# Second attention: DVE instead of ACT copies each pair's output out of PSUM, first in every odd slot

## The reference, cut to what matters

```
scores = jnp.einsum('bhqd,bhkd->bhqk', q, k_h) / math.sqrt(HEAD_DIM)
scores = jnp.where(causal[None, None], jnp.finfo(scores.dtype).min, scores)
attn = jax.nn.softmax(scores, axis=-1)
ctx = jnp.einsum('bhqk,bhkd->bhqd', attn, v_h)
ctx = ctx.transpose(0, 2, 1, 3).reshape(b, t, D_OUT)
```

## Time and profile before

| | us |
|---|---|
| median of three runs | 1215.43 |
| the profiled execution | 1214.89 |
| its span in the trace | 1213.3 |
| PE busy in the span | 1180.8 (97%) |
| PEld busy | 1023.2 (84%) |
| DVE busy | 799.6 (66%) |
| ACT busy | 752.5 (62%) |
| POOL busy | 548.3 (45%) |

### The profile page before, as it was taken

How to read it: one execution, slowest core, us unless ns; L and a number is a source line. 1 busy time by engine, 2 the same in 40 slices (tenths; PEclk the granted TensorE clock), 3 DMA queues, 4 the chain that set the end, 5 groups by cost and what they waited for, 6 DMA issues and landing times. The chain is left out here.

```text
span 1213.3 us, 21135 instructions
## 1 busy us (share of the span) xinstructions
PE 1180.8 (97%) x6698; PEld 1023.2 (84%) x6698; DVE 799.6 (66%) x2575; ACT 752.5 (62%) x1758; POOL 548.3 (45%) x519
## 2 busy tenths in 40 slices
PE   7899999999999999999999999999999999999997
PEld 6788888888888888888888788888887999999886
DVE  6757776667766677766777722223458888888685
ACT  6656765566655567655665454441129999999624
POOL 4554454444533554534533233331136766676400
PEclk9999999999999999999999999999999999999999
DMA  6011110011110111101000022220002213220001
GB/s 223 18 44 36 35 36 28 22 43 27 46 34 12 44 36 35 36 27 35 27 1 27 18 70 78 61 97 1 18 20 53 65 41 108 48 48 21 1 1 70
DMA packets 30368, 51.28 MB, mean 42 GB/s; under 512 B 5680, under 2 KB 6576, under 8 KB 30256
## 3 DMA queue, kind: packets, MB, share of 16 engines
q1 hardware_dynamic: 29680, 48.85, 13.7%
q10 hardware_dynamic: 576, 1.05, 0.2%
HBM read 38.35 MB, written 2.10 MB: 33 GB/s over the span
## 5 line engine op out<-in xcount | busy, mean ns | idle before, releaser
L487 POOL TENSOR_TENSOR turned<-turned,sin 128x512 f32<-128x512 f32 x73 | 94.4, 1293 | 311.5 <-ACT turned L347 311.5
L363 ACT ACTIVATE probs<-probs,neg_max 128x256 f32<-128x256 f32 (+1 forms) x256 | 119.8, 473 | 14.0 <-DVE neg_max L580 14.0
L1484 ACT ACTIVATE a_probs<-a_probs,a_neg_max 128x512 f32<-128x512 f32 (+3 forms) x256 | 123.2, 571 | 0.1
L1720 DVE CUSTOM_DVE_ANT_0 a_probs<-bank,a_mask 128x512 f32<-128x512 f32 (+3 forms) x256 | 109.7, 485 | 0.2 <-PE bank L1949 0.2
L490 POOL TENSOR_TENSOR turned<-turned,by_cos 128x512 f32<-128x512 f32 x73 | 101.1, 1385 | 5.7
L96 PE MATMUL bank<-wo_hi,oT_hi 128*128 128x512 f32 x256 | 100.3, 392 | 1.7 <-DVE oT_lo L643 1.7
L734 PE MATMUL bank<-xT_hi,wq_hi 128*128 128x512 f32 x256 | 101.7, 397 | 0.0
L734 PE MATMUL bank<-xT_lo,wq_hi 128*128 128x512 f32 x256 | 100.2, 391 | 0.0
L734 PE MATMUL bank<-xT_hi,wq_lo 128*128 128x512 f32 x256 | 100.1, 391 | 0.0
L96 PE MATMUL bank<-wo_hi,oT_lo 128*128 128x512 f32 x256 | 99.9, 390 | 0.0
L96 PE MATMUL bank<-wo_lo,oT_hi 128*128 128x512 f32 x256 | 99.7, 389 | 0.0
(11 more groups left out here) (239 smaller groups left out, 3454.0 us busy)
## 6 DMA issues: line engine op xcount, KB each, us to landing
staged<-weights SPq DMA_DIRECT2D x70, 256.0 KB, 2.7
f_staged<-weights_f SPq DMA_DIRECT2D x33, 256.0 KB, 2.7
a_q_stack<-a_qT_hi SPq DMA_DIRECT2D x64, 64.0 KB, 2.0
rows<-x_rows SPq DMA_DIRECT2D x2, 1024.0 KB, 7.4
a_k_stack<-a_kT_hi SPq DMA_DIRECT2D x64, 32.0 KB, 2.0
a_q_stack<-a_qT_lo SPq DMA_DIRECT2D x32, 64.0 KB, 2.0
out<-rows SPq DMA_DIRECT2D x8, 256.0 KB, 2.0
a_raw<-weights_qkv SPq DMA_DIRECT2D x4, 384.0 KB, 4.9
```

The source lines that it names most:

```text
L363: act.activation(probs[:, s % 2, h, 0:width], probs[:, s % 2, h, 0:width], ACT.Exp, bias=neg_max[:, s % 2, h:h + 1], scale=SCALE0, accum_o ...
L487: pool.tensor_tensor(at, at, sin[:, :], ALU.mult).then_inc(sin_done, 1)
L1484: act.activation(row_probs(s, qt), row_probs(s, qt), ACT.Exp, bias=neg_max[:, h, qt:qt + 1], scale=-1.0).then_inc(exp_done, 1)
L1720: dve.tensor_tensor_reduce(row_probs(s, qt), ps_s[bank][:, at:at + seen], mask[:, SEQ - seen:SEQ], -SCALE1, HIGHEST, ALU.add, ALU.min, neg ...
```

## The change

The copy of the output from PSUM leaves ACT's list and enters DVE's. On ACT it stood first in each odd slot from 3 to 65, on DVE it does so too: ahead of `maxima(s+2)`, with the same two waits and the same signal. There are 32 copies, as before. No other line changes.

```diff
@@ block.scalar
-            def evacuate(n):
-                act.wait_ge(applied, 2 * (n + 1))
-                if n >= 1:
-                    act.wait_ge(o_turned, n)
-                act.activation(oT_now[:, :], ps_o[:, :], ACT.Copy).then_inc(o_read, 1)
-
             for s in range(SLOTS1 + 2):
                 u, h = divmod(s, GROUP1)
-                if s % 2 == 1 and s >= 3:
-                    evacuate((s - 3) // 2)
                 if s + AHEAD_EXPS < SLOTS1:
                     exps(s + AHEAD_EXPS)
@@ block.vector
+            def evacuate(n):
+                dve.wait_ge(applied, 2 * (n + 1))
+                if n >= 1:
+                    dve.wait_ge(o_turned, n)
+                dve.tensor_copy(oT_now[:, :], ps_o[:, :]).then_inc(o_read, 1)
+
             for s in range(SLOTS1 + 2):
+                if s % 2 == 1 and s >= 3:
+                    evacuate((s - 3) // 2)
                 if s + AHEAD_MAXIMA < SLOTS1:
                     maxima(s + AHEAD_MAXIMA)
```

## The result

The changed kernel takes 1208.36 us (median of 4 executions, 1207.41 to 1208.94), the kernel before 1215.38 beside it. The ratio is 0.9939 with an interval of 0.9922 to 0.9956: faster by 7.0 us. Two later sets of the same changed kernel gave 1207.16 (5 executions, 1206.83 to 1208.14; ratio 0.9933, 0.9920 to 0.9947) and 1206.96 (5 executions, 1206.80 to 1207.28; ratio 0.9932, 0.9919 to 0.9945), so the gain is nearer to 8 us: the medians lie 8.4 and 8.2 us under those of the kernel before beside them, 1215.57 and 1215.19. Beside the third set two slow executions, 3581.15 us of the kernel before and 1460.18 us of the kernel with the later weights, are left out of the medians. The first profiled execution has a span of 1207.2 us, the one of the first repeat 1205.5.

A forecast was written before the change was run, and what follows sets the result against it. ACT's list was taken to set 6.68 us per pair, with PE's floor of 6.47 next. Minus 6.2 for the main stretch, minus 0.9 for the loop's end and nothing for the opening gave -7.1, 1208.3 us, range 1205.5 to 1212.5.

The forecast's parts named there:

- ACT set the pace: Second attention's loop: ACT, needing 6.6 to 6.7 us per pair of slots without waiting, sets the 6.68 us period.
- PE's floor: Second attention's loop: PE's pair without waits takes 6.47 us, so at most 0.21 of ACT's 0.50 can be had.
- The term of -6.2: Slots 7 to 61: 27 pairs at 6.47 give minus 6.6 us, with 0.4 left to POOL's weight splitting.
- The copy's price on DVE: DVE's 128x512 PSUM copy: row 650 ns, 0.57 us of queue, bringing DVE to 6.31 us per pair.
- The slack: Copy ahead of the maxima on DVE: signalled by 5.95 us, needed by PE's apply at 6.47, 0.5 us of slack.
- The loop's end: Turn of slot 61 to apply in slot 63: 7.75 us falls to 6.6, 0.2 given back to POOL, minus 0.9.
- The opening: First slots: ACT loses a 0.50 us copy, DVE gains 0.57; counted as nothing, 0.6 us either way.
- DVE as the bound: Rival: DVE's queue sets the pair at 6.54 us, giving 1210.2 us, or 1214 with more waiting; chance 0.16.
- PE waiting for the copy: Rival: DVE's copy runs 1.10 us, DVE needs 6.91 per pair, 5.4 us lost, 1220.8 us; chance 0.05.
- PE's floor lower: Rival: idle weight loads, 0.45 us per pair, can mostly be had, DVE's 6.31 is next, 1204.1 us; chance 0.06.
- Nothing changes: Rival: something other than ACT's load, such as the circle apply, POOL, apply, sets 6.68; 1214 to 1216 us; chance 0.05.
- The rule weighed: DVE's queue: by the drain rule the copy costs its whole 0.65 us, DVE 6.39; by the trace 0.57 and 6.31.

The follow-up runs named there:

- the kernel with the later weights: Changed kernel with only POOL's splitting of output weights moved from slots 2-5 and 10-13 to 5, 6, 8, 9, 11, 12, 14, 15: 1206.77 us.
- the second experiment: Changed kernel with DVE copying 128x256 more from PSUM in each join, result unused: 1213.68 us, ratio 0.9994.
- the first experiment: Changed kernel with an unused 128x512 SBUF copy on ACT where the output copy stood, DVE keeping its copy: 1213.93 us, ratio 0.999.
- the narrow copy: Kernel before with ACT's output copy cut to 32 of 512 columns in all pairs but the first: 1209.14 us, ratio 0.9947.
- the early copy and the later weights: Changed kernel with the first output copy issued at slot 2 and POOL's output-weight splitting moved to slots 5 to 15: 1206.73 us, ratio 0.9928.

## Why the prediction held, point by point

**ACT set the pace.** Right. Loading ACT again gives back 6.67 per pair, relieving it on the kernel before without touching DVE gives 6.45, and relieving it further on the changed kernel gives nothing in the main stretch. One reading was too strict: ACT's list did wait a little. Its own sum is 6.56 or, with the value copy, 6.70 per pair, and in the pairs without it the copy of the output starts late for its `apply` (the roundings ahead of the copy at 1027.38 start at 1026.52, 0.86 earlier, and take 0.74). So 6.63 of the 6.68 was ACT's work.

**PE's floor.** Right: 6.47 was added up from rows with their waits taken off, and the undisturbed pairs are 6.45 to 6.49, 6.457 in the mean. The 27 pairs take 174.73, forecast 174.7 with 0.4 on top for the weight slots. That 0.4 was right: slots 10 to 13 wait for nothing, but slot 49 waits 0.37 (0.45 in the kernel before) and its pair takes 6.86 instead of 6.46. It was the floor that was 0.013 too high, times 27 pairs 0.35. The term of -6.2 should have been -6.5, or -6.4 by the repeats (174.90 and 174.89).

**The copy's price on DVE.** A little low: the row is 681 ns long, forecast 650, and takes 0.60 of the queue, forecast 0.57, so that DVE's own work is 5.74 + 0.60 = 6.34 and not 6.31. Adding the two-operand instruction's 1.07 ns per element to the copy of 128 columns came out under the truth; at 512 columns the copy costs what the two-operand instruction does (688), which was my nearest row from above. The wait ahead of the join is 0.09 (forecast 0.15).

**The slack.** Right: 0.5 by the layout, 0.56 in the rows. The layout is also what the position hangs on: moving the copy behind the maxima turned the gain into a loss of 2.6%.

**The loop's end.** Right in kind, and 0.2 small: -1.07, forecast -0.9. PE's last `apply` rows wait 0.29 for the copy and 0.28 for POOL; I had them at 0.2.

**The opening.** Counted at nothing with 0.6 either way, measured -0.45. This is the largest term that I left out. The wait that I should have seen, 1.07 for the first copy, is there, but it takes the place of 1.71 of other waits.

**The sum.** -7.1 forecast; -8.06 by the stages and -8.4 by the medians of the first repeat (1215.57 to 1207.16). The error by the stages is 0.3 from the floor, 0.2 from the end and 0.45 from the opening. That the first median is 0.06 from the forecast is luck: the late start of slot 0 in the profiled execution (1208.79, and by its time of 1208.94 perhaps one more) stands against these three. By the medians of the two repeats the true distance is 1.1 to 1.3 us.

**The rivals.** DVE as the bound: not reached, but by 0.11 per pair and not by 0.16; the second experiment shows what an addition of 0.33 costs. PE waiting for the copy from a row of 0.9 on: the rows are 0.68, and all 32 lie between 679 and 692 ns, so the five slow rows didn't carry over. PE's floor lower: the pair didn't go below 6.45 with ACT or DVE relieved. There remain (123.10 - 118.27) / 19 = 0.25 of idle loads per pair that no run here used. The Trainium skill, Perfetto Trace Analysis, section "Identifying the Most-Contended Engine", has TensorE judged by its weight loads' busy share; here 93% did mean room, but more than half of what was missing to 100% (6.8% of the window before, 3.9% after) stays when PE is the bound. Nothing changes: excluded by the result, and ACT's load as what set the 6.68 is shown by the first experiment and the narrow copy.

**The signs that were named.** Turns 6.47 to 6.55 apart: they are 6.45 to 6.49 but for the pair from slot 49 to 51, 6.86, so a little better. No wait ahead of `apply` outside the weight slots: yes. ACT idle 0.3 to 0.4 per pair: seen as 0.24 to 0.3, and only in every second pair, since the value copy stands in the others. DVE near 95% busy: it is 99%. The forecast's own 6.31 of 6.47 was already 98%, and the tail of the row ahead of the join covers the wait of 0.09.

**The rule weighed.** A copy of 0.68 lets the next instruction start after 0.60, and one of 0.42 after 0.33. By the Trainium skill, VectorE: DVE Perf Modes, section "The DRAIN you can't avoid", the next operation doesn't start until the pipeline is empty; the same section adds that a next operation that isn't held starts earlier. The traces agree with the addition: the next start comes 0.08 to 0.09 before the row's end. With the copy's row counted whole DVE's pair of 6.34 would have been 6.42, still under PE's floor.

## What to carry to other kernels

When two engines both look full, add up the start-to-start distances of each with its waits taken off; the engine whose sum equals the period sets it, and the next sum says how much can be had (here 0.2 of a 0.5 us copy per pair). Before moving work to an engine with idle time, lay out one period and find the slack of that very instruction at the place in the list where it goes: the same copy one step later in DVE's list cost 38.6 us (1246.99 against 1208.36). A wait that appears after a change isn't a loss until the waits that it replaced are counted, and one execution's start can hide or feign more than a microsecond, so compare stages as well as spans.

## What the runs showed of the hardware that was not expected

ACT's rows grow when its list never waits, with no change in what they take of the queue. In the first experiment the raw copy of 128x512 starts with rows of 0.58 us at the loop's start, has 0.95 to 0.99 in the pair shown and grows to 1.13, against 0.60 in the changed kernel; four exponentials have 2.30 against 1.92. The distances from start to start stay at 0.47 and 1.82. So the length of such a row isn't a price in that list, and only the distance is.

The copy of 128x512 out of PSUM on DVE takes 681 ns, that of 128x256 takes 415 and that of 128x128 takes 239: 1.38 ns per element in the first step and 1.04 in the second, so a line through two of the three points misses the third. The smallest one reads 16 of every 64 numbers and the others read without gaps, so whether width or stride bends the line isn't shown.

TensorE's clock at the opening differs between executions of one kernel. Of the thirteen profiled executions seven have one stretch at a granted clock of 0.50 between 46 and 54 us, two have it at 56 to 59 us (the first of the changed kernel, and the one with the early copy and the later weights), and four have none there. Slot 0 begins at 913.46 to 914.21 in the eleven without the late stretch, and at 915.40 and 915.57 in the two with it, some 1.6 us later in a time of 1207. The changed kernel alone gave both places.
